# First attention scores two heads at a time on the two halves of TensorE's rows, with the steps of the attention loop in another order

## The chip, the core and the metric

The kernel runs on one core of a Trainium2 chip. The metric is the device time of one execution in microseconds (us). TensorE multiplies matrices and writes PSUM, VectorE (DVE) and ScalarE (ACT) read PSUM and work on rows, GpSimd (POOL) does small vector work, SyncE (SP) issues most DMA transfers. Each engine takes its instructions in program order and waits on semaphores.

## The reference

The block is an adaptive layer norm around an attention layer with an MLP, and then one around a mixture of experts. Cut to what matters here (B = 8 sequences of S = 512 tokens, D = 128, H = 16 heads of 8 elements):

```python
h = _layernorm(x) * (1 + ca) + sa                     # ca, sa, ... from silu(c) @ wmod
x = x + ga * attn_layer(h)                            # ga, gb: clipped gates
h = _layernorm(x) * (1 + cb) + sb
x = x + gb * ffn(h)                                   # shared expert + top 2 of 8 experts

# attn_layer
x = _layernorm(hidden_states, ln1_g, ln1_b)
Q = einsum('bsd,dhr,hre->bhse', x, q_U, q_V) + q_b    # K, V alike
scores = einsum('bhse,bhte->bhst', Q, K) * scale
scores = where(causal, scores, -1e9)
attn = softmax(scores, axis=-1)
ctx = einsum('bhst,bhtd->bhsd', attn, V)
h = hidden_states + ctx @ out_U @ out_V + out_b
return h + gelu(_layernorm(h) @ fc1_U @ fc1_V + fc1_b) @ fc2_U @ fc2_V + fc2_b
```

## The kernel before

**The whole program.** A setup (about the first 42 us of the span) loads and multiplies out the weights and normalises the first three sequences. The attention follows, up to about 381 us. Then come the MLP, the router and the scatter of tokens to expert slots, up to about 538 us, and at last the experts. The diff touches the setup and the attention.

**The attention loop.** A group is 4 of the 16 heads of one sequence, and there are 32 groups (`NG`). Step n works on three groups at once: `s1(n + 3, ...)` makes the first scores of group n+3, `s2(n, ...)` makes the second, transposed scores of group n, and `context(n - 1, ...)` multiplies the probabilities of group n-1 with V. Steps -3, -2 and -1 hold first scores alone, and steps 29 and up hold none. The loops run over `n` in `range(FIRST_STEP, MERGE)` on every engine.

**First scores.** Q and K are each split into bf16 parts, six products are stacked, so that one score is a contraction over 48 rows (`SROWS`). The stacks of Q (`q_st`) and of K (`k_st`) lie on partitions 0 to 47 for one head and 64 to 111 for another. A unit of `S1_UNITS` is one PSUM bank of queries i (128 of them) by all keys up to i: two heads each in units 0 to 3 (128 or 256 keys), one head in units 4 to 11 (384 or 512 keys). For each unit TensorE first writes the causal mask (`ident_b` times `later_q`, L1245) and then adds the scores (L1248), both over all 128 rows: the other head's rows of `q_st` are zero. VectorE takes the row maximum of the bank (`take_max`, L1669). GpSimd splits the negated maxima into three bf16 rows (`split_max`, L831 to L839), TensorE transposes them (`transpose_max`, L1254), ScalarE copies them out (`empty_max`, L1020), and SP stores them to `max_d` (L597) and loads them into three more rows of `q_st` (L607), a step and more ahead of their use.

**Second scores.** `s2(n, u)` has six units, each two PSUM banks of `ps_s2`, and its matmuls stand on 64 rows each: one head on the lower half, one on the upper half, with their own bank (mask L1272, scores L1276). The added rows subtract the maximum. ScalarE takes the exponential of both banks (`exp_unit`, L989). `context` (L1293) uses 32 columns of the array for each of four heads.

**The ring.** The first scores share three PSUM banks (`ps_r`, a ring) with the transposed maxima ("M"), the transposed input ("T"), the projections ("Q", "K", "V"), the output projection ("O") and the transposed rows after attention ("U"). `ring_order` writes the order by hand; entry k lies in bank k modulo 3, and `bank` makes TensorE wait until the entry three places earlier has been read, by VectorE (`max_taken`), or by ScalarE (`act_emptied`). So a bank that ScalarE is late with holds up first scores.

**The other work of a step** goes by n modulo 4, one sequence in four steps: TensorE does O and K in one step, V in the next, U in the next, T and Q in the last. VectorE does one or two parts of the layer norms in each step (`layer_norm`, after units 3 and 7), and adds O after unit 3. `gates` (L1563 and on) works out the gates ga and gb on VectorE after step -3. SP's queue holds, in each step, in this order: the loads of stacks for a coming sequence, `load_ctx`, `store_max`, the stores of stacks, `store_ctx`, `load_max`, `move_rec`. In step 27 (`EARLY_STEP`) SP issues the loads that the MLP and the experts need (L671 to L679).

## Time and profile before

| | us |
|---|---|
| median of three runs | 706.72 |
| lowest and highest of the three | 703.84, 706.77 |
| the profiled execution, its own time | 706.39 |
| its span, first to last instruction | 704.6 |

The granted clock of TensorE was 0.98 over the span. The profile lists for each engine the time in which it was busy. The rows of a timeline are instructions in order of time; consecutive ones of a kind are merged (x4), and the bracket tells how long the engine was idle before and what ended it. A matmul's duration has a fixed part in it, so what one costs in a sequence is read from the distance between the starts. Of the idle reasons, "issue" is time in which the engine waited for nothing that the profile shows.

### The profile page before, as it was taken

The numbers are of one execution on the slowest core, as the hardware profiler recorded it, in microseconds if no ns is written. First come the engines' busy times: TensorE is split into PE (matmuls) and PEld (weight loads), VectorE is DVE, ScalarE is ACT, GpSimd is POOL, SyncE is SP. The second block draws the span as 40 slices with busy tenths as digits, with TensorE's granted clock in tenths as the row PEclk, the third lists the DMA queues.
The fourth block names the chain that finished last, engine by engine and source line by source line (L and its number), as shares of the span: only waits on it lengthen the run. The fifth ranks groups of instructions, "written<-read, shape, count | busy, mean of one in ns | idle before, by whom it ended". The sixth has DMA issues, their size and how long they took to land.

```text
span 704.6 us, 15442 instructions
## 1 busy us (share of the span) xinstructions
PE 633.6 (90%) x5389; PEld 416.6 (59%) x5389; DVE 447.6 (64%) x1346; ACT 409.1 (58%) x720; POOL 301.7 (43%) x480
## 2 busy tenths in 40 slices
PE   4977899999999999999978886999998999999997
PEld 3543444444444544444434575766766999999993
DVE  5749887878788776767742878777673222222227
ACT  4432667676676767666666565676434555555550
POOL 4232424243442524232313438766771545455452
PEclk9999999999999999999999998999899999999999
DMA  9552332443343344332463511211236777777769
GB/s 212 189 177 74 118 102 87 144 138 113 109 153 102 126 140 136 131 106 72 132 189 108 143 36 50 81 51 50 70 96 197 205 239 222 221 224 225 234 209 322
DMA packets 86125, 100.97 MB, mean 143 GB/s; under 512 B 13008, under 2 KB 68216, under 8 KB 85952
## 3 DMA queue, kind: packets, MB, share of 16 engines
q1 hardware_dynamic: 76896, 87.19, 40.3%
q0 software_dynamic: 4544, 9.45, 3.7%
q10 hardware_dynamic: 4608, 3.35, 1.8%
q8 instruction: 43, 0.70, 0.4%
q14 instruction: 34, 0.28, 0.1%
HBM read 60.28 MB, written 37.57 MB: 139 GB/s over the span
## 4 chain that ended last, share of the span: by engine, by line
PE 53%; DVE 14%; DMA 9%; ACT 8%; SPq 6%; issue 5%; POOL 4%; POOLq 0%; ACTq 0%; DVEq 0%
PE ps_pv L1293 9%; PE ps_r L1478 7%; PE ps_s L1468 6%; DVE row_max L1669 6%; PE ps_r L1248 5%; PE ps_r L1245 4%; DMA arena<-slots_d 4%; PE ps_pv L1364 4%; PE ps_s L1276 3%; POOL slots_d L910 3%; PE ps_r L1223 2%; PE ps_s L1272 2%; PE ps_s L1372 2%; ACT arena L1081 2%; DMA arena<-in_w_mod 1%
## 5 line engine op out<-in xcount | busy, mean ns | idle before, releaser
L1669 DVE TENSOR_REDUCE row_max<-ps_r 128x1 f32<-128x384 f32 (+3 forms) x384 | 206.9, 595 | 63.1 <-PE ps_r L1248 61.8
L989 ACT ACTIVATE arena<-ps_s 128x1024 f32<-128x1024 f32 (+1 forms) x192 | 159.3, 881 | 70.8 <-PE ps_s L1276 69.8
L1248 PE MATMUL ps_r<-arena 128*128 128x384 bf16 (+3 forms) x512 | 118.7, 303 | 0.0
L956 POOL DMA_INDIRECT y_d<-arena,target x78 | 74.9, 960 | 87.7 <-DVE arena L1878 75.5
L1245 PE MATMUL ps_r<-later_q,ident_b 128*128 128x128 bf16 (+1 forms) x384 | 91.4, 244 | 22.0 <-DVE row_max L1669 15.8
L1245 PEld LDWEIGHTS ps_r<-later_q,ident_b 128*128 128x128 bf16 x384 | 35.9, 97 | 84.1 <-DVE row_max L1669 42.4
L1874 DVE TENSOR_TENSOR arena<-ps_r,arena_early 128x256 f32<-128x256 f32 x39 | 16.6, 425 | 108.2 <-PE ps_r L1478 108.2
L1293 PE MATMUL ps_pv<-arena 128*32 128x512 f32 (+3 forms) x1024 | 83.3, 443 | 0.1
L910 POOL DMA_INDIRECT slots_d<-arena,slots x64 | 65.5, 1023 | 18.2 <-issue 18.2
L1276 PE MATMUL ps_s<-arena 51*128 51x256 bf16 (+3 forms) x512 | 59.9, 298 | 0.0
L1478 PEld LDWEIGHTS ps_r<-arena 128*128 128x128 f32 x480 | 58.2, 192 | 1.5
L1144 ACT ACTIVATE arena<-ps_s,arena 128x256 f32<-128x256 f32 x120 | 50.4, 471 | 13.9 <-PE ps_s L1468 13.2
L1478 PE MATMUL ps_r<-arena 128*128 128x128 f32 x480 | 58.3, 275 | 0.0
L1248 PEld LDWEIGHTS ps_r<-arena 128*128 128x128 bf16 x512 | 50.6, 99 | 12.8 <-issue 2.4
L1468 PE MATMUL ps_s<-arena 128*128 128x256 f32 x240 | 56.8, 379 | 0.0
L831 POOL TENSOR_SCALAR neg_part<-row_max 128x16 bf16<-128x16 f32 x32 | 8.3, 260 | 89.0 <-DVE row_max L1669 89.0
L1293 PEld LDWEIGHTS ps_pv<-arena 128*32 128x32 f32 x1024 | 27.0, 110 | 32.2 <-issue 25.8
L1468 PEld LDWEIGHTS ps_s<-arena 128*128 128x128 f32 x240 | 43.3, 190 | 4.6
L1272 PE MATMUL ps_s<-ident_h,lower_k 64*128 64x64 bf16 (+1 forms) x384 | 39.9, 204 | 5.2 <-ACT arena L989 4.7
L1102 ACT ACTIVATE arena<-ps_s,cols 128x512 f32<-128x512 f32 x32 | 21.6, 686 | 31.6 <-PE ps_s L1372 30.9
L770 POOL TENSOR_TENSOR var_eps<-moments,ln_eps 128x4 f32<-128x4 f32 x24 | 4.9, 203 | 79.9 <-DVE moments L1494 79.9
L1272 PE MATMUL ps_s<-ident_h,upper_k 64*128 64x64 bf16 (+1 forms) x384 | 38.7, 198 | 0.0
(236 smaller groups left out, 1129.1 us busy)
## 6 DMA issues: line engine op xcount, KB each, us to landing
arena<-in_ew SPq DMA_DIRECT2D x30, 514.0 KB
ctx_d<-ctx_raw SPq DMA_DIRECT2D x32, 256.0 KB, 3.1
arena<-q_d SPq DMA_DIRECT2D x64, 102.0 KB
arena<-k_d SPq DMA_DIRECT2D x64, 96.0 KB
arena<-slots_d SPq DMA_DIRECT2D x39, 132.0 KB, 3.1
arena_early<-in_ew SPq DMA_DIRECT2D x9, 514.0 KB
arena<-y_d SPq DMA_DIRECT2D x8, 512.0 KB, 6.0
q_d<-arena_early SPq DMA_DIRECT2D x8, 384.0 KB, 2.9
```

What stands on the lines that cost most here:

```text
L910: pool.indirect_dma_start(slots_d[:], bass.IndirectOffsetOnAxis(ap=slots[:, c, i:i + 1], axis=0), n3x[:, c, i, :], None).then_inc(scattere ...
L956: pool.indirect_dma_start(y_d[:], bass.IndirectOffsetOnAxis(ap=target[:, k, c:c + 1], axis=0), res[:, k, c, :], None).then_inc(put[k], 16)
L989: act.activation(dst, src, ACT.Exp, scale=SCALE).then_inc(exp_done, 1)
L1144: act.activation(x_hidden[:, k, f], ps_s2[:, 2 * (k % 2) + f // 2, (f % 2) * SLOTS:(f % 2 + 1) * SLOTS], ACT.Relu, bias=x_w[k][:, FF + NF ...
L1245: pe.matmul(diag, ident_b[:], later_q[:].unsqueeze(1).to_broadcast([P, len(js), P]), start=True, stop=False, skip_group_check=True)
L1248: mm = pe.matmul(bnk[:, k * keys:(k + 1) * keys], q_st[b % 2][:, g, j, i * P:(i + 1) * P], k_st[b % 2][:, g, j // 2, 0:keys], start=False, ...
L1272: pe.matmul(banks[half][:, :, at:at + HALF], stationary[whole], near, start=(at == 0), stop=False, skip_group_check=True)
L1276: mm = pe.matmul(banks[j % 2][:, k // 2, :], k_st[b % 2][rows, g, j // 2, kt * P:(kt + 1) * P], q_st[b % 2][rows, g, j, kt * P:S], start=F ...
L1293: mm = pe.matmul(ps_pv[32 * j:32 * j + 32, kt * P:S], v_sb[b % 2][:, kt, GROUPS * j + g, :], probs[:, p % 2, at:at + length], start=(kt == ...
L1468: mm = pe.matmul(ps_s2[:, 2 * (k % 2) + f // 2, (f % 2) * SLOTS:(f % 2 + 1) * SLOTS], x_w[k][:, f * P:(f + 1) * P], tok_t[:, k], start=Tru ...
L1478: mm = pe.matmul(ps_s1[:, k % 2, c * P:(c + 1) * P], x_hidden[:, k, f, c * P:(c + 1) * P], x_w[k][:, FF + f * D:FF + (f + 1) * D], start=( ...
L1669: dve.reduce_max(row_max[:, m % 2, js[0] % 2, j:j + len(js), i], src, AXIS.X).then_inc(max_taken, 1)
```

## The change

**First scores in pairs.** `s1` now makes two units at once, one on the rows 0 to 63 and one on the rows 64 to 127 of the array, each into its own bank of the ring. The mask is made of four products on 64 rows (`ident_h` with the two parts of a wider `later_q`), the scores follow by turns of the two halves. `q_st` holds no zero rows any longer (`JH` becomes 2), so that their clearing on ScalarE, on SP's queue (two DMAs of `zeros`) and the wait for both fall away.

**Ring and places.** "M" leaves the ring for a corner of `ps_s2` (bank 3), and so do V, Q and K of all sequences but the first, and U of the first six (`beside`, the right half of the banks 2 and 3). Products beside the ring wait in `place_of` for what lay there, and the unit 1 of the second scores waits until ScalarE has emptied them. T stands after the units 4 and 5, O after 6 and 7.

**Order of a step.** Each pair of first scores is followed by one unit of the second scores and a part of the context. ScalarE's, VectorE's (layer norm after units 1, 3, 7 and 9, O after 7) and GpSimd's orders follow, the roots (`x_rstd_of`, `h_rstd_of`) now ahead of K's remainder. `gates` moves into VectorE's setup.

**Unread products.** `fill_in` issues two products of 512 bf16 columns ahead of each pair in the steps -3 to -1; nobody reads them.

```diff
+def beside(name, b):
+    return b is not None and (name == "V" or name in "QK" and b > 0 or name == "U" and GROUPS * b + AFTER_T_AT < NG)
...
-        units(m, 0, 1)
-        one(n, "O")
-        units(m, 2, 3)
-        if 0 <= m - 1 < NG:
-            order.append(("M", m - 1))
-        units(m, 4, 5)
-        one(n, "T", "K", "V")
-        units(m, 6, 7)
-        one(n, "Q")
-        units(m, 8, 9, 10, 11)
-        if batch_at(n, AFTER_T_AT) is not None:
-            order.append(("U", batch_at(n, AFTER_T_AT)))
+        units(m, 0, 1, 2, 3, 4, 5)
+        one(n, "T")
+        units(m, 6, 7)
+        one(n, "O")
+        units(m, 8, 9)
+        one(n, *(name for name in "QKU" if not beside(name, batch_at(n, AT[name]))))
+        units(m, 10, 11)
...
-        q_st = [first.take(GROUPS, JH, S, dt=BF16) for k in range(2)]
+        q_st = [first.take(GROUPS, 2, S, dt=BF16) for k in range(2)]
...
+            def home(name, b):
+                if beside(name, b):
+                    return ps_s2[:, 2:4, S // 2:S]
+                return ring(name, b).rearrange("p (c s) -> p c s", c=2)
...
-                    for k in range(2):
-                        sp.dma_start(q_d[k, len(PRODUCTS)].rearrange("p (c s) -> p c s", c=2),
-                                     zeros[:].bitcast(BF16).unsqueeze(1).to_broadcast([P, 2, S // 2])).then_inc(zero_rows, 16)
...
-                    for stack in q_st:
-                        act.activation(stack[:].rearrange("p g j s -> p (g j s)").bitcast(F32), zeros[:, 0:1].to_broadcast([P, GROUPS * JH * S // 2]), ACT.Copy)\
...
+                    def place_of(name, b):
+                        if not beside(name, b):
+                            bank(name, b)
+                            return home(name, b)
+                        n = GROUPS * b + AT[name]
+                        pe.wait_ge(small_copied, 4)
+                        wait(pe, act_emptied, beside_until(n))
+                        wait(pe, max_copied, min(n + LAG, NG))
+                        wait(pe, exp_done, NS2 * n + 4)
+                        return home(name, b)
...
+                    def fill_in(n):
+                        if -LAG <= n < 0:
+                            for k in range(2):
+                                pe.matmul(ps_pv[:].rearrange("p (c s) -> p c s", c=NT), ident_b[:],
+                                          lower_q.unsqueeze(1).to_broadcast([P, NT, P]), start=True, stop=True)
...
-                            bnk = bank("S", n)
-                            keys = P * (i + 1)
-                            diag = bnk[:, 0:len(js) * keys].rearrange("p (j s) -> p j s", j=len(js))[:, :, keys - P:keys]
-                            pe.matmul(diag, ident_b[:], later_q[:].unsqueeze(1).to_broadcast([P, len(js), P]), start=True, stop=False,
-                                      skip_group_check=True)
+                            banks = [bank("S", NS1 * m + u + half)[:, 0:len(js) * keys].rearrange("p (j s) -> p j s", s=keys) for half in range(2)]
+                            for stationary, at in ((lower_q, keys - P), (upper_q, keys - HALF)):
+                                for half in range(2):
+                                    whole = slice(HALF * half, HALF * half + HALF)
+                                    near = ident_h[whole].unsqueeze(1).to_broadcast([HALF, len(js), HALF])
+                                    pe.matmul(banks[half][:, :, at:at + HALF], stationary[whole], near, start=(at == keys - P), stop=False,
+                                              skip_group_check=True)
                             for k, j in enumerate(js):
-                                mm = pe.matmul(bnk[:, k * keys:(k + 1) * keys], q_st[b % 2][:, g, j, i * P:(i + 1) * P],
-                                               k_st[b % 2][:, g, j // 2, 0:keys], start=False, stop=True, skip_group_check=True)
-                            mm.then_inc(s1_done, 1)
+                                for half in range(2):
+                                    rows = slice(HALF * half, HALF * half + SROWS)
+                                    mm = pe.matmul(banks[half][:, k, :], q_st[b % 2][rows, g, j // 2, i * P:(i + 1) * P],
+                                                   k_st[b % 2][rows, g, j // 2, 0:keys], start=False, stop=True, skip_group_check=True)
+                                    if k == len(js) - 1:
+                                        mm.then_inc(s1_done, 1)
...
+                        if u == 1:
+                            wait(pe, max_copied, min(n + LAG - 1, NG))
+                            wait(pe, act_emptied, beside_until(n))
...
-                        s2(n, 0)
-                        s2(n, 1)
-                        context(n - 1, 0)
-                        s1(m, 0, 1)
+                        fill_in(n)
+                        s1(m, 0, 1)
+                        s2(n, 0)
+                        context(n - 1, 0)
+                        fill_in(n)
+                        s1(m, 2, 3)
+                        s2(n, 1)
+                        context(n - 1, 1)
...
                     normalise_all(2)
+                    gates()
...
-                            if u in (3, 7):
+                            if u in (1, 3, 7, 9):
                                 layer_norm(n, u)
...
-                        if n == MOD_STEP - 1:
-                            gates()
```

**TensorE at the head of a step, before.** `ps_s` is `ps_s2`, `arena` the stacks or probabilities; `128x64` is the output tile, and the bracket holds what the instruction waits for. The rows are a step's first two units of the second scores, the first part of the context and the first unit of first scores.

```order
L1272 MATMUL ps_s<-ident_h,lower_k 128x64 [waits exp_done,max_loaded1]
...
L1276 MATMUL ps_s<-arena 128x512 x2
L1272 MATMUL ps_s<-ident_h,lower_k 128x64 [waits exp_done]
...
L1276 MATMUL ps_s<-arena 128x512 x2
L1293 MATMUL ps_pv<-arena 32x512 [waits act_emptied,ctx_out,exp_done]
...
L1245 MATMUL ps_r<-later_q,ident_b 128x256 [waits max_taken,st_loaded0]
L1248 MATMUL ps_r<-arena 128x128 x2
```

The same place now, the second step of a sequence:

```order
L1289 MATMUL ps_r<-ident_h,later_q 128x2x64 [waits max_taken,st_loaded1]
...
L1294 MATMUL ps_r<-arena 128x128 x4
L1330 MATMUL ps_s<-ident_h,later_k 128x64 [waits exp_done,max_loaded0]
...
L1334 MATMUL ps_s<-arena 128x512 x2
L1351 MATMUL ps_pv<-arena 32x512 [waits ctx_out,exp_done]
...
L1289 MATMUL ps_r<-ident_h,later_q 128x2x64 [waits max_taken]
...
L1294 MATMUL ps_r<-arena 128x256 x4
L1330 MATMUL ps_s<-ident_h,later_k 128x64 [waits act_emptied,max_copied,exp_done]
```

A pair of first scores now stands ahead of each single unit of the second scores, and the second of these waits for ScalarE's emptying too.

**TensorE around the transposed maxima and K's or V's projection, before.** L1254 transposes the maxima, L1229 is V's projection.

```order
L1254 MATMUL ps_r<-ident_b,neg_part 48x128 [waits max_taken,max_split]
L1245 MATMUL ps_r<-later_q,ident_b 128x128 [waits max_taken]
L1248 MATMUL ps_r<-arena 128x384
...
L1229 MATMUL ps_r<-w_qkv,arena_early 128x128 [waits act_emptied]
...
L1276 MATMUL ps_s<-arena 128x256 x4
...
L1276 MATMUL ps_s<-arena 128x128 x4
L1245 MATMUL ps_r<-later_q,ident_b 128x128 [waits act_emptied]
L1248 MATMUL ps_r<-arena 128x512
```

Now (L1308 transposes the maxima, L1264 is V's projection):

```order
L1308 MATMUL ps_s<-ident_b,neg_part 48x128 [waits exp_done,act_emptied,max_copied,max_split]
...
L1334 MATMUL ps_s<-arena 128x384 x2
...
L1294 MATMUL ps_r<-arena 128x512 x2
...
L1334 MATMUL ps_s<-arena 128x256 x4
L1264 MATMUL ps_s<-w_qkv,arena_early 128x128 [waits exp_done,max_copied,act_emptied,small_copied]
...
L1289 MATMUL ps_r<-ident_h,later_q 128x64 [waits max_taken]
...
L1294 MATMUL ps_r<-arena 128x512 x2
...
L1334 MATMUL ps_s<-arena 128x128 x4
```

The maxima and the projection write `ps_s` in place of `ps_r`; the first scores behind the projection no longer wait for ScalarE.

**TensorE ahead of the first of all first scores, before** (L1223 is Q's or K's projection of the second sequence, L1203 the bias of the output):

```order
L1223 MATMUL ps_r<-arena_early,w_qkv 128x512 [waits act_emptied]
L1203 MATMUL ps_r<-w_out,arena 128x128 [waits act_emptied,small_copied]
L1245 MATMUL ps_r<-later_q,ident_b 128x256 [waits st_loaded0,v_ones,act_emptied,mod_copied,small_copied]
L1248 MATMUL ps_r<-arena 128x128 x2
L1245 MATMUL ps_r<-later_q,ident_b 128x256 [waits dve_emptied]
```

Now:

```order
L1257 MATMUL ps_s<-arena_early,w_qkv 128x256 [waits small_copied,act_emptied]
...
L1223 MATMUL ps_r<-w_out,arena 128x128 [waits act_emptied,small_copied]
L1257 MATMUL ps_s<-arena_early,w_qkv 128x256 [waits act_emptied,small_copied]
...
L1271 MATMUL ps_pv<-later_q,ident_b 128x512 [waits v_ones,mod_copied,small_copied]
...
L1289 MATMUL ps_r<-ident_h,later_q 128x2x64 [waits act_emptied,st_loaded0]
...
L1294 MATMUL ps_r<-arena 128x128 x4
```

K's projection now waits for ScalarE to empty Q's, since both lie in the same place, and two unread products stand ahead of the pair.

## Rows read from the trace of the kernel before

**Rows 1.** The page, first part, and busy time by stretch (two of attention, its end):

```profile
PE 633.6 (90%) x5389; PEld 416.6 (59%) x5389; DVE 447.6 (64%) x1346; ACT 409.1 (58%) x720; POOL 301.7 (43%) x480
...
180.00:200.00 20.00, 19.06 (x207) 9.20 (x206) 15.89 (x39) 14.83 (x24) 10.09 (x16) 1.00 0.41 137
200.00:220.00 20.00, 18.06 (x218) 9.39 (x214) 17.22 (x49) 11.97 (x18) 6.25 (x17) 1.00 0.37 124
...
360.00:380.00 20.00, 15.57 (x207) 6.99 (x199) 1.67 (x5) 14.52 (x21) 3.54 (x4) 0.91 0.40 131
```

**Rows 2.** The chain that ended last: the context's later parts in steps 1, 8, 18, 27:

```profile
81.30 1.43 PE ps_pv L1293 x24
...
150.78 1.43 PE ps_pv L1293 x24
...
253.26 1.43 PE ps_pv L1293 x24
...
342.17 1.43 PE ps_pv L1293 x24
```

**Rows 3.** Waits between 80 and 270 us: engine line, waited for, us, times, longest:

```profile
DVE row_max L1669 <- PE ps_r L1248: 34.8, 55, 1.8
...
PEld ps_r L1245 <- DVE row_max L1669: 21.8, 46, 1.1
```

**Rows 4.** Timeline of TensorE, first scores: two units of 256, two of 512 keys:

```profile
190.86 0.27 PE L1245 MATMUL ps_r<-later_q,ident_b 128*128 128x256 bf16 x1
...
191.19 0.27 PE L1245 MATMUL ps_r<-later_q,ident_b 128*128 128x256 bf16 x1
...
196.74 0.23 PE L1245 MATMUL ps_r<-later_q,ident_b 128*128 128x128 bf16 x1 [0.26 <-ACT arena_early L1005]
...
197.02 0.22 PE L1245 MATMUL ps_r<-later_q,ident_b 128*128 128x128 bf16 x1
```

**Rows 5.** Timeline of TensorE, second scores: starts of units in the same steps:

```profile
195.75 0.23 PE L1272 MATMUL ps_s<-ident_h,lower_k 64*128 64x128 bf16 x2
...
196.09 0.22 PE L1272 MATMUL ps_s<-ident_h,lower_k 64*128 64x128 bf16 x2
...
198.35 0.20 PE L1272 MATMUL ps_s<-ident_h,lower_k 64*128 64x64 bf16 x2
...
198.64 0.19 PE L1272 MATMUL ps_s<-ident_h,lower_k 64*128 64x64 bf16 x2
```

**Rows 6.** Timeline of TensorE, from second scores to the context:

```profile
198.70 0.38 PE L1276 MATMUL ps_s<-arena 51*128 51x512 bf16 x2
...
199.01 1.06 PE L1293 MATMUL ps_pv<-arena 128*32 128x512 f32 x8
```

**Rows 7.** Timeline of VectorE, the twelve maxima of one step:

```profile
349.43 0.76 DVE L1669 TENSOR_REDUCE row_max<-ps_r 128x2 f32<-128x256 f32 x2 [0.73 <-PE ps_r L1248]
350.93 1.29 DVE L1669 TENSOR_REDUCE row_max<-ps_r 128x2 f32<-128x512 f32 x2 [0.74 <-PE ps_r L1248]
...
353.73 4.57 DVE L1669 TENSOR_REDUCE row_max<-ps_r 128x1 f32<-128x384 f32 x8 [0.92 <-PE ps_r L1248]
```

**Rows 8.** Timeline of GpSimd in steps 23 and 24:

```profile
310.11 1.28 POOL L857 TENSOR_TENSOR ctx_n<-ctx_t,rec_rows 128x512 f32<-128x512 f32 x1 [6.89 <-DMA rec_rows<-rec_d]
...
315.08 0.25 POOL L839 TENSOR_SCALAR neg_part<-neg_left 128x16 bf16<-128x16 f32 x1
```

**Rows 9.** Timeline of SP's queue from step 27 on:

```profile
344.10 0.32 SPq L597 DMA_DIRECT2D max_d<-max_rows  x1
...
347.12 6.69 SPq L673 DMA_DIRECT2D arena_early<-mod_d  x3
353.85 1.65 SPq L675 DMA_DIRECT2D arena_early<-in_router_t  x1
...
357.51 0.83 SPq L597 DMA_DIRECT2D max_d<-max_rows  x1
...
362.61 0.58 SPq L607 DMA_DIRECT2D arena<-max_d  x2
```

**Rows 10.** Waits between 340 and 384 us:

```profile
PEld ps_s L1272 <- DMA arena<-max_d: 3.0, 1, 3.0
```

**Rows 11.** Timeline around VectorE's gates, in the steps of first scores alone:

```profile
53.80 0.52 DVE L1574 SCALAR_TENSOR_TENSOR arena<-arena 8x128 f32<-8x128 f32 x2
...
54.72 0.28 PE L1245 MATMUL ps_r<-later_q,ident_b 128*128 128x256 bf16 x1 [1.57 <-DVE row_max L1669]
```

## What is expected of the change

> **What bounds the kernel now.** I read four views in this order.
>
> First the page and the busy time by stretch: in the attention TensorE is busy for 19.06 and 18.06 of 20 us, VectorE for 15.89 and 17.22, ScalarE for less, and the clock is granted in full (1.00) [rows 1]. So TensorE is nearly full and VectorE is close behind: (15.89 + 17.22) / 40 = 0.83 of the time.
>
> Second the chain, which gives the length of a step: the context's later parts start at 81.30 us in step 1, 150.78 in step 8, 253.26 in step 18 and 342.17 in step 27 [rows 2]. That is 69.5 / 7 = 9.93 us a step, then 102.5 / 10 = 10.25, then 88.9 / 9 = 9.88. VectorE's work is thus 0.83 x 10.25 = 8.5 us in the middle steps. In the last ones, which have no input norms, it is at least its twelve maxima, 0.76 + 1.29 + 4.57 = 6.6 us [rows 7]. That the steps hardly became shorter when the input norms ended shows that TensorE sets their length.
>
> Third the waits: between 80 and 270 us VectorE waits for first scores for 34.8 us, and TensorE's first scores for VectorE for 21.8 us [rows 3]. Both happen, since the work comes in lumps: neither engine is saturated all the time.
>
> Fourth SP's queue. In step 27 it issues loads for the later phases from 347.12 us on (6.69 and 1.65 us for two of them). The store of maxima behind them goes out at 357.51 and their load at 362.61 [rows 9], and TensorE waits 3.0 us for it [rows 10]. From there on the queue sets the pace.
>
> Everything behind the attention (some 325 us) is untouched, and starts when the attention ends.
>
> **The change part by part.** The sum is made against the profiled execution's own time, 706.39 us (span 704.6); that is 0.33 us under the median of the three runs, so the same sum holds for both.
>
> *First scores in pairs.* A unit of 256 keys takes 191.19 - 190.86 = 0.33 us for 768 columns, one of 512 keys 0.28 us for 640 [rows 4], so 0.43 ns a column. A step's twelve units have 7168 columns: 3.1 us. A pair now has just the shape of a unit of the second scores, and those run two heads side by side already: 0.34 us with 256 keys (two matmuls on each half and the masks), 0.29 us with 512 [rows 5]. The 384 key pairs by the same rate take 0.23, the 128 key pair 0.25. Six pairs: 0.25 + 0.34 + 2 x 0.23 + 2 x 0.29 = 1.6 us. TensorE is relieved of 1.5 us a step.
>
> *More changes of shape.* The array goes between 128 rows, 64 rows and 32 columns. The second 512-column pair starts at 198.70, streams for 0.21, and the context starts at 199.01 [rows 6]: a gap of 0.10 us. Before, a step has 8 such changes; now the second scores follow the first without one, but the context is cut into three, and the maxima, O and the projections stand alone: some 10.7. That costs 0.27 us a step. The Trainium skill, page "TensorEngine Tiling (Array Packing)", section "Key Properties", says that changing the tiling mode drains TensorE. By that rule, the trace agrees, with 0.10 us. It speaks against this part of the change.
>
> Net relief on TensorE: 1.2 us a step. The steps 0 to 26 can pass it on (27 steps, 32 us at most); from 27 on the queue decides.
>
> *What is late next.* In the middle steps (8 to 17) TensorE needs 10.25 - 1.2 = 9.05, VectorE 8.5. They meet at short distance now: a pair takes two of three banks, so TensorE can start the next pair when VectorE has read the first bank of the last one, and no sooner. Behind the first pair stand one unit (0.29), the context's longest part (1.06, [rows 6]), two changes (0.2) and the next pair (0.34), 1.9 us, while VectorE has 0.76 of maxima and some 0.6 of norm: it idles for about 0.5. T or O in the ring costs about as much again in every second step. 8.5 + 0.5 + 0.3 = 9.3. Taken: 9.3, a gain of 0.95 in 10 steps. Bounds: 8.5 (VectorE full) and 10.25 (nothing).
>
> *Sum over the steps.* Steps 0 to 7: 8 x 1.2 = 9.6. Steps 8 to 17: 10 x 0.95 = 9.5. Steps 18 to 26, VectorE relieved of the input norms: 9 x 1.2 = 10.8. Together 29.9 us.
>
> *GpSimd's chain.* In steps 23 and 24 GpSimd waits for the reciprocals' rows until 310.11, does three operations of 1.3 us, and has the maxima split at 315.08 + 0.25 [rows 8]. This hangs on SP's queue, not on TensorE. With shorter steps the transposition comes first and waits: -2.5 us. Elsewhere the same chain ends some 3 us sooner and is covered.
>
> *The steps of first scores alone.* These three run at VectorE's pace. The gates leave it there, ending at 53.80 + 0.52, for which TensorE had waited 1.57 us [rows 11]; they now fall into the setup, where VectorE waited for TensorE anyway. The unread products (2 x 512 columns, 0.43 us a pair at the rate above, 0.86 at half clock) run while VectorE reads two banks (0.76 to 1.3 us): nothing, or 0.2 a pair if the clock is low. Against it K's projection now waits for Q's emptying, and the first pair starts about 1 us later. Together +0.5, between -3 and +3.
>
> *Edits at nothing.* The two clearings of `q_st` on ScalarE and the two DMAs of zeros lie beside weight loads that come sooner in the queue. The emptying of Q, K, V and U (up to 1.4 us) comes after the last exponential, and the second unit that waits for it stands some 2 us into the next step: hidden. If it is not, it costs what is over in each step. M out of the ring frees first scores from ScalarE. The roots ahead of K's remainder: 1.2 us on GpSimd, which is idle more than half the time.
>
> *From step 27 on.* Maxima of the last groups, SP's loads, store, load: 344.10 to 364 us stays as it is, and a faster loop only reaches it sooner. No gain and no loss.
>
> 29.9 - 2.5 + 0.5 = 27.9. 706.4 - 27.9 = 678.5; taken 679.
>
> **The rivals.**
>
> *The exchange of banks takes most of it.* If each of the six pairs, not only the first, lets VectorE idle for 0.25 us, a middle step takes 8.5 + 1.5 = 10.0, and the others gain 0.3: 27 x 0.28 = 7.5, so 699. For it: the 34.8 us of VectorE's waits now, with up to three banks of lead [rows 3]. Against it: TensorE has 1.2 us less to do, and the norms are spread over four places. The Trainium skill, the same page, section "PSUM Bottleneck", says that after a speedup of TensorE the reading of PSUM may become the bottleneck; by that rule, the trace agrees with 0.83 for VectorE.
>
> *Chains through SP and GpSimd take a part.* The 2.5 us come in each sequence, or the emptying of Q and K holds the second unit: -10 in all, 689.
>
> *The waits vanish as well.* Order and work are spread evenly, VectorE is full in the middle (8.6), and the late steps fall to 8.0: 8 x 1.9 + 10 x 1.65 + 9 x 1.9 = 49 at the utmost; 45 less gives 661.
>
> *Slower: the clock falls.* TensorE has less to do in a step, and the clock is granted at half (1.2 GHz) after it has waited: the stretch with the 3.0 us wait shows 0.91, and the attention, whose waits end at 1.8 us, shows 1.00 [rows 1, 3, 10]. A step's 8.4 us of TensorE would take 16.8 at half clock, 7.5 more than 9.3. Four of 27 steps at half clock eat the gain; that is the point from which it decides. Seven of them: 679 + 52 = 731. Against it: what is left idle comes in pieces of under 1 us.
>
> *Pairs do not overlap.* Then first scores stay at 3.1 or more and the changes of shape and the 24 mask products add 0.4 us a step: 706.4 + 11 = 717. The second scores speak against it [rows 5].
>
> **How the numbers follow.** Forecast (672 to 686) 0.50; exchange of banks (690 to 703) 0.17; chains (686 to 696) 0.10; waits vanish (656 to 670) 0.12; clock 0.08; no overlap 0.03. The range reaches from 662, in the middle of the fourth, to 700, over the second: about 0.8. A measurement of this kernel can tell about 0.5% (3.5 us) from no change. Faster by more: 0.50 + 0.15 + 0.10 + 0.12 = 0.87; within: 0.04; slower: 0.09.
>
> **What would show it.** In the profile after: starts of 512 key pairs 0.29 us apart from what follows, halves at the same time; six context starts a step with 0.1 us gaps; steps of 8.7, 9.3 and 8.7 us; VectorE busy over 0.9 in the middle steps; a granted clock of 1.00 from 65 us on; one wait of 2 to 3 us of the transposed maxima for GpSimd about step 24; the wait for the loaded maxima in step 30 as before or longer. Wrong would be: VectorE's waits for first scores over 1.5 us a step (the exchange of banks), second scores waiting for ScalarE's emptying, or a clock under 1.00 in the loop.

## The result

Twenty executions of the changed kernel took 705.01 us in the median (693.1 to 712.0), twenty of the kernel before on the same chip 706.78 (703.8 to 713.2). The changed kernel's executions spread more widely, and the comparison leaves out those more than 1.5% above the fastest of a kernel, eleven of the changed kernel's twenty and none of the other's: by it the changed kernel takes 0.9877 of the time before, interval 0.985 to 0.990, some 9 us less. A later comparison on another chip gave 0.9874 (0.984 to 0.991), with medians of all its executions of 700.6 and 708.9 us, so the gain does not hang on which executions are counted. The forecast was 679 us, 28 us less, with 662 to 700 as the range: the direction was right, the size was three times too large.

The profiled execution took 706.2 us and lies above its own median. A second one, of the later comparison, has a span of 697.8 us. What is read below stands in both, unless it says otherwise. Line numbers of the changed kernel: first scores L1289 (masks) and L1294, second scores L1330 and L1334, context L1351, transposed maxima L1308, maxima on VectorE L1735, reciprocals L1758.

The page of the changed kernel (busy time; the clock in 40 slices), and busy time by stretch, whose last columns are granted clock, DMA share and GB/s; they answer to [rows 1]:

```profile
PE 607.5 (86%) x5841; PEld 401.2 (57%) x5841; DVE 450.2 (64%) x1346; ACT 408.1 (58%) x718; POOL 301.2 (43%) x478
...
PEclk9999799999999989998989988999899999999999
...
180.00:200.00 20.00, 18.23 (x252) 9.12 (x246) 16.56 (x41) 15.62 (x23) 10.54 (x17) 0.95 0.43 140
200.00:220.00 20.00, 17.20 (x267) 8.64 (x265) 18.73 (x52) 14.44 (x21) 6.41 (x17) 1.00 0.38 124
360.00:380.00 20.00, 13.16 (x164) 4.92 (x168) 1.28 (x4) 14.13 (x20) 1.08 (x1) 0.83 0.36 124
```

TensorE is busy for 26 us less, and in an undisturbed stretch (200 to 220 us) VectorE is busy for 18.73 of 20 us. But the clock is under 1.00 in stretches of the loop, which it was not before.

TensorE's timeline in step 13, two pairs and the context behind the first (answers to [rows 4 to 6]):

```profile
196.40 0.29 PE L1289 MATMUL ps_r<-ident_h,later_q 64*128 64x128 bf16 x4 [0.65 <-DVE row_max L1735]
...
196.62 0.24 PE L1330 MATMUL ps_s<-ident_h,later_k 64*128 64x64 bf16 x4
196.68 0.40 PE L1334 MATMUL ps_s<-arena 51*128 51x512 bf16 x2
197.01 1.06 PE L1351 MATMUL ps_pv<-arena 128*32 128x512 f32 x8
...
204.29 0.23 PE L1289 MATMUL ps_r<-ident_h,later_q 64*128 64x64 bf16 x4
...
204.58 0.28 PE L1330 MATMUL ps_s<-ident_h,later_k 64*128 64x128 bf16 x4
```

A pair of 128 keys takes 196.62 - 196.40 = 0.22 us until the second scores behind it start, a pair of 512 keys 204.58 - 204.29 = 0.29. The prediction had 0.25 and 0.29. The gap at the change of shape ahead of the context is again 0.1 us.

The waits between 80 and 270 us (answers to [rows 3]):

```profile
PEld ps_r L1289 <- DVE row_max L1735: 48.6, 72, 4.3
...
DVE row_max L1735 <- PE ps_r L1294: 20.9, 36, 2.1
...
DVE recs L1758 <- DMA sums<-ctx_d: 7.4, 3, 3.7
```

TensorE, by the rows of its weight loads (`PEld`), now waits for VectorE for 48.6 us instead of 21.8, once for 4.3. VectorE waits less for TensorE, 20.9 instead of 34.8. The third row is new in size: the reciprocals' wait for the context's sums was 2.4 us between 80 and 330 us before, at most 0.9 at once. (In the second execution it is 3.9 between 80 and 270 us, at most 2.0.)

The steps tell the rest. By the starts of the context (L1351, 128x512), 18 of the steps 1 to 27 of the profiled execution take 8.4 to 9.7 us; but step 1 takes 10.1, step 11 13.7, step 19 15.7, step 24 12.3. In the second execution other steps are long: step 7 13.2, step 12 12.4, step 24 12.3. Here is step 19, SP's queue, then VectorE, then TensorE, in the first execution:

```profile
247.68 0.54 SPq L609 DMA_DIRECT2D arena<-q_d  x1
...
253.18 0.60 SPq L612 DMA_DIRECT2D arena<-k_d  x1
253.88 0.57 SPq L646 DMA_DIRECT2D sums<-ctx_d  x1
...
251.98 0.69 DVE L1735 TENSOR_REDUCE row_max<-ps_r 128x1 f32<-128x512 f32 x1 [0.32 <-PE ps_r L1294]
256.38 0.55 DVE L1758 RECIPROCAL recs<-sums 128x64 f32<-128x64 f32 x1 [3.71 <-DMA sums<-ctx_d]
...
257.95 0.39 PE L1289 MATMUL ps_r<-ident_h,later_q 64*128 64x128 bf16 x4 [3.46 <-DVE row_max L1735]
259.24 1.50 PE L1351 MATMUL ps_pv<-arena 128*32 128x384 f32 x8
```

SP issues eight loads of the stacks, from 247.68 on, before it issues the load of the sums at 253.88. VectorE meets the reciprocals early, since steps are shorter, and stands for 3.71 us with a maximum behind it. TensorE's pair waits for that maximum for 3.46 us. Then the context's second part takes 1.50 us instead of 0.85: the clock is at half (1.2 GHz). So a load on SP's queue, which the prediction had read from step 27 on alone, costs a step some 6.5 us.

### The profile page after: what moved, and what is told of

It is laid out like the page before. It is cut to its first block, busy times and chain, and to the rows that moved or that the text cites. A ratio compares the mean times of both kernels' runs of the same rounds, so it can differ in the third digit from the quotient of the medians.

```text
span 704.5 us, 16609 instructions
## 1 busy us (share of the span) xinstructions
PE 607.5 (86%) x5841; PEld 401.2 (57%) x5841; DVE 450.2 (64%) x1346; ACT 408.1 (58%) x718; POOL 301.2 (43%) x478
## 4 chain that ended last, share of the span: by engine, by line
PE 46%; DMA 13%; DVE 12%; SPq 9%; issue 9%; ACT 6%; POOL 5%; POOLq 0%; ACTq 0%; DVEq 0%
PE ps_r L1543 7%; PE ps_s L1533 7%; PE ps_pv L1351 6%; DVE row_max L1735 6%; PE ps_pv L1429 4%; DMA arena<-slots_d 3%; PE ps_r L1289 3%; POOL slots_d L931 3%; PE ps_r L1294 3%; DMA k_d<-arena_early 2%; DMA arena<-y_d 2%; PE ps_s L1334 2%; SPq L612 2%; PE ps_s L1437 2%; SPq L609 2%
## 5 line engine op out<-in xcount | busy, mean ns | idle before, releaser
L1735 DVE TENSOR_REDUCE row_max<-ps_r 128x1 f32<-128x384 f32 (+3 forms) x384 | 211.4, 594 | 45.8 <-PE ps_r L1294 43.1
L1007 ACT ACTIVATE arena<-ps_s 128x1024 f32<-128x1024 f32 (+1 forms) x192 | 168.6, 882 | 86.8 <-PE ps_s L1334 85.1
L1351 PE MATMUL ps_pv<-arena 128*32 128x512 f32 (+3 forms) x1024 | 95.4, 471 | 0.0
L1289 PEld LDWEIGHTS ps_r<-ident_h,later_q 64*128 64x128 bf16 x768 | 24.7, 94 | 121.3 <-DVE row_max L1735 78.9
L1289 PE MATMUL ps_r<-ident_h,later_q 64*128 64x64 bf16 (+1 forms) x768 | 49.5, 206 | 42.7 <-DVE row_max L1735 42.3
L1938 DVE TENSOR_TENSOR arena<-ps_r,arena_early 128x256 f32<-128x256 f32 x39 | 16.6, 425 | 108.2 <-PE ps_r L1543 108.2
L1294 PE MATMUL ps_r<-arena 48*128 48x384 bf16 (+3 forms) x512 | 70.8, 310 | 0.0
L1334 PE MATMUL ps_s<-arena 51*128 51x256 bf16 (+3 forms) x512 | 70.6, 310 | 0.0
L1164 ACT ACTIVATE arena<-ps_s,arena 128x256 f32<-128x256 f32 x120 | 50.4, 471 | 13.8 <-PE ps_s L1533 13.2
L1330 PE MATMUL ps_s<-ident_h,later_k 64*128 64x64 bf16 (+1 forms) x768 | 49.2, 204 | 6.0 <-ACT max_rows L1038 4.9
L1330 PEld LDWEIGHTS ps_s<-ident_h,later_k 64*128 64x128 bf16 x768 | 35.9, 98 | 25.1 <-ACT arena L1007 10.2
L1351 PEld LDWEIGHTS ps_pv<-arena 128*32 128x32 f32 x1024 | 24.3, 111 | 29.9 <-issue 16.5
L878 POOL TENSOR_TENSOR ctx_n<-ctx_t,rec_rows 128x512 f32<-128x512 f32 x8 | 10.2, 1275 | 61.7 <-DMA rec_rows<-rec_d 61.7
```

What stands on the lines that cost most here:

```text
L1007: act.activation(dst, src, ACT.Exp, scale=SCALE).then_inc(exp_done, 1)
L1164: act.activation(x_hidden[:, k, f], ps_s2[:, 2 * (k % 2) + f // 2, (f % 2) * SLOTS:(f % 2 + 1) * SLOTS], ACT.Relu, bias=x_w[k][:, FF + NF ...
L1289: pe.matmul(banks[half][:, :, at:at + HALF], stationary[whole], near, start=(at == keys - P), stop=False, skip_group_check=True)
L1294: mm = pe.matmul(banks[half][:, k, :], q_st[b % 2][rows, g, j // 2, i * P:(i + 1) * P], k_st[b % 2][rows, g, j // 2, 0:keys], start=False, ...
L1330: pe.matmul(banks[half][:, :, at:at + HALF], stationary[whole], near, start=(at == 0), stop=False, skip_group_check=True)
L1334: mm = pe.matmul(banks[j % 2][:, k // 2, :], k_st[b % 2][rows, g, j // 2, kt * P:(kt + 1) * P], q_st[b % 2][rows, g, j // 2, kt * P:S], st ...
```

## The experiments

The theory after these rows: every undisturbed step gains about what was forecast. The gain is given back at waits behind orders written for longer steps (SP's queue, GpSimd's), and each wait is made dearer by a clock that falls behind it. The main rival: the clock falls because pairs leave TensorE less busy, whatever waits.

**Loads in another order.** The load of the sums moves ahead of the stack loads in SP's step, in the changed kernel and in the kernel before:

```
+                        if batch_at(n, CTX_AT) is not None:
+                            load_ctx(batch_at(n, CTX_AT))
                         for g, later in ((0, 0), (1, 0), (2, 1), (3, 2)):
...
-                        if batch_at(n, CTX_AT) is not None:
-                            load_ctx(batch_at(n, CTX_AT))
```

> The changed kernel with one edit: SP's queue issues the context's loads (load_ctx) ahead of the eight loads of stacks in the same step. Theory Q (the queue): in the changed kernel VectorE waits at its reciprocal for the sums (2.8, 3.7 and 2.4 us in steps 10, 18 and 22), the last two maxima of the step stand behind it, TensorE waits for those, and the granted clock falls after it. By Q these three waits and the falls behind them go: the contexts' starts in steps 11/12 and 19/20 lie under 10 us apart, not 13.7 and 15.7, and the ratio to the kernel before falls from 0.988 to 0.970 to 0.978. Rival C (the clock falls by itself, from TensorE's smaller load): the waits go, but the steps still hold stretches at half clock, and the ratio stays at 0.983 or above.

> The kernel before with the same edit of SP's queue. Theory Q: there the sums came in time (waits of 0.3 us), so the edit changes nothing: ratio 0.997 to 1.003. Rival (the queue's order was a cost in both kernels): ratio under 0.995.

Measured: 0.9851 (0.980 to 0.990) for the changed kernel, 1.0037 (1.001 to 1.007) for the one before. Step 19 falls to 10.4 us and the reciprocals wait no more. But step 15 now takes 14.5, the clock is at half for as long as before (41 us between 60 and 380 us), and the ratio is the one that the rival had named (0.983 or above). The kernel before became slightly slower with the edit. In the changed kernel with that order, ScalarE and TensorE:

```profile
220.77 0.60 ACT L1043 ACTIVATE ctx_raw<-ps_pv 128x512 f32<-128x512 f32 x1 [3.26 <-DMA ctx_d<-ctx_raw]
...
222.09 0.29 PE L1289 MATMUL ps_r<-ident_h,later_q 64*128 64x64 bf16 x4 [3.23 <-ACT arena_early L1014]
```

The store of the context now stands at the end of the longer row of transfers; ScalarE's copy waits for it, the emptying of T behind the copy, and TensorE behind that. So the queue's order as a whole has to be tested.

**SP's order mended.** The store of the context goes ahead of the loads too:

```
                         if batch_at(n, CTX_AT) is not None:
                             load_ctx(batch_at(n, CTX_AT))
+                        if 0 <= n - 2 < NG:
+                            store_ctx(n - 2)
                         for g, later in ((0, 0), (1, 0), (2, 1), (3, 2)):
```

> The changed kernel, in which SyncE issues in each step first the load of the context's row sums, then the store of the context of two steps before, and only then the stack loads, the maxima's store and load. Theory (each undisturbed step is won, and the gain is lost again to waits behind an in-order queue, each of about 3 us, that drag the granted clock down after them): with the loads first gone, the stall moved from step 19 (15.7 us) to step 15 (14.5 us), because the context's store then stood behind a longer row of transfers; with the store ahead too, both should be gone: no step but 12, 24 and those from 29 on over 11 us, TensorE's longest wait on VectorE and on ScalarE's x_t copy under 1.5 us each between 90 and 300 us, half clock in the loop 25 to 35 us instead of 40.8, ratio to the kernel before 0.975 to 0.985. Rival (the clock falls because pairs leave TensorE less busy, whatever waits): half clock stays at 35 us or more, ratio 0.985 to 0.990, as with the loads first alone (0.9851).

Measured: 0.9763 (0.971 to 0.982), 690.6 us. Both stalls are gone: steps 1 to 27 take 8.2 to 11.5 us, and TensorE's longest wait for VectorE between 80 and 330 us is 1.6, where it was 3.5. By the records of the granted clock, the attention loop runs 20 us at half instead of 41. TensorE's work is the same, so the falls that went stood behind the waits. The rival is not refuted: the clock still falls for 6.8 us in step 0 and for 3.4 us at 133 us, where no wait is long.

**GpSimd's order.** The addition of the output bias moves a step earlier: `batch_at(n, 3)` becomes `batch_at(n, 2)`.

> The changed kernel, with GpSimd's addition of the output bias (line 900) in the step before, instead of the step whose GpSimd work also holds the normalised context and the addition of fc2's bias, and whose splitting of the maxima it delays. Theory: the transposition of the negated maxima no longer waits 2.6 us in step 24 but under 1, step 24 takes 9 to 10.5 us instead of 12.4 and the half clock behind it (6.8 us from 313 us on) goes; step 19 stays at about 15.7 us; ratio 0.981 to 0.986, 1 to 4 us less than the changed kernel. Rival (the bias addition is not what delays the split, the load of the reciprocals is): step 24 over 11.5 us, ratio 0.986 to 0.989.

Measured: 0.9824 (0.978 to 0.987), which overlaps the interval of the changed kernel without the move. Step 24 takes 10.4 us instead of 12.3, though step 23 took 12.7, behind a wait of 3.0 us for the sums, and step 19, which was expected to stay long, took 9.9. What the move takes away is seen in step 12 of the changed kernel's second execution, GpSimd, then TensorE:

```profile
184.62 1.28 POOL L878 TENSOR_TENSOR ctx_n<-ctx_t,rec_rows 128x512 f32<-128x512 f32 x1 [7.78 <-DMA rec_rows<-rec_d]
185.86 1.27 POOL L893 TENSOR_TENSOR h_sb<-h_sb,fc_bias 128x512 f32<-128x512 f32 x1
187.10 1.27 POOL L900 TENSOR_TENSOR h_sb<-h_sb,out_bias 128x512 f32<-128x512 f32 x1
...
189.61 0.25 POOL L860 TENSOR_SCALAR neg_part<-neg_left 128x16 bf16<-128x16 f32 x1
...
189.92 0.24 PE L1308 MATMUL ps_s<-ident_b,neg_part 128*48 128x128 bf16 x1 [1.34 <-POOL neg_part L860]
```

This is the chain of [rows 8], and in the changed kernel it reaches TensorE in step 12 as well, where before it was covered.

**All moves, in both kernels, and a third.** To both moves comes `EARLY_STEP = NG - 6` (SP's loads for the later layers in step 26).

> The changed kernel with three moves: SyncE's order of the run before this one, GpSimd's addition of the output bias one step earlier, and SyncE's loads for the later layers in step 26 instead of 27. Theory: the three causes of lost gain are gone together; no step from 1 to 26 over 11 us, 27 steps in 250 to 256 us (before 271, changed kernel 266), half clock inside the loop under 20 us, and the tail from step 27 on 2 to 5 us shorter; ratio to the kernel before 0.955 to 0.970. Rival (the clock falls by lighter load): half clock in the loop stays above 35 us, ratio 0.975 to 0.985. Rival 2 (SyncE's queue is full in the tail wherever the loads stand): the tail's long steps only move, ratio 0.970 to 0.978.

> The kernel before with the same three moves. Theory (the queue order costs only since the steps have become shorter): steps 1 to 26 as before, since its waits there were hidden behind TensorE; ratio 0.990 to 1.003, the part below 1 from the earlier loads in the tail and the transposition that waited for GpSimd in step 24. Rival (the moves are good by themselves, whatever the pairs do): ratio 0.975 to 0.985, so that the gap between the two kernels stays at 1.2% under the same moves.

Measured: 0.9731 (0.969 to 0.978) and 1.0069 (1.005 to 1.009). The third move was a miss: step 28, which stands behind its loads, took 15.0 us in the changed kernel and 16.6 in the kernel before. (Step 20 of the changed kernel took 14.6, behind GpSimd's chain, whose rows came 10.1 us late; that step lies six steps ahead of the moved loads.) SP's queue in the changed kernel with the three moves:

```profile
333.67 6.73 SPq L696 DMA_DIRECT2D arena_early<-mod_d  x3
...
350.24 0.57 SPq L630 DMA_DIRECT2D arena<-max_d  x2
```

The maxima that now stand behind the loads are needed sooner. Without the third move, and with it one step later instead:

> The changed kernel with the two moves that each gained alone: SyncE issues the load of the context's sums and the store of the context ahead of the stack loads (0.9763 alone), and GpSimd adds the output bias one step earlier (0.9824 alone); the loads for the later layers stay in step 27. Theory: what SyncE's order left, the transposition that waits for GpSimd in steps 12 and 24 (10.7 and 11.2 us), goes to 9 to 10 us; no step from 1 to 27 over 11 us; ratio to the kernel before 0.965 to 0.975, 1 to 6 us under SyncE's order alone, and below the three moves together (0.9731), whose loads in step 26 made steps of 14.6 and 15.0 us. Rival (the two moves take away the same time): ratio 0.974 to 0.980.

> The kernel before with SyncE's and GpSimd's moves alone, without the earlier loads that made one step of 16.6 us in the kernel before with all three. Theory (the moves pay only where steps are shorter): ratio 0.994 to 1.004, so that the paired scores under the same moves are worth 2.0 to 3.0% instead of 1.2%. Rival (the moves are good in themselves): ratio 0.980 to 0.990.

> The kernel with the two moves, and SyncE's loads for the later layers in step 28 instead of 27. Theory (the row of loads takes 6 to 7 us of SyncE's queue wherever it stands, and the maxima's transfers behind it hold up the steps from 29 on): the long step moves by one and keeps its 11 to 15 us, or moves behind the last load of maxima, where nothing waits for it; the time is within 3 us of the two moves alone, on either side. Rival (the loads cost only where maxima still have to be moved): 3 to 6 us less than with the two moves.

The changed kernel with the two moves takes 0.9737 (0.970 to 0.977), 689.8 us; the kernel before with the same two 1.0012 (0.998 to 1.005). So the two moves are worth 1.4% in the changed kernel and nothing in the one before: what they take away was hidden there. So the third move changed nothing in the changed kernel's time (0.9731 against 0.9737): it moved the long step. With the late loads in step 28 the ratio is 0.978 (0.975 to 0.981), and step 30 takes 12.9 us instead of 8.0: the queue's load of the maxima is late one step further on.

**The clock at the start.** In step 0 of the changed kernel TensorE waits 0.3 to 1.3 us ahead of each pair, and the clock falls:

```profile
60.00:80.00 20.00, 15.44 (x158) 7.90 (x158) 17.69 (x43) 8.68 (x14) 6.01 (x14) 0.82 0.25 79
...
73.08 0.29 PE L1289 MATMUL ps_r<-ident_h,later_q 64*128 64x64 bf16 x4 [1.26 <-DVE row_max L1735]
...
75.72 2.05 PE L1257 MATMUL ps_s<-arena_early,w_qkv 128*128 128x256 f32 x4
```

Three runs with fewer or more unread products. The first is the changed kernel without them; the second the changed kernel with one more ahead of each pair in all steps from 0 on, into the pair's first bank; the third has the two products in step 0 too, on top of the two moves:

```
 # first                       # third
-if -LAG <= n < 0:            -if -LAG <= n < 0:
+if False:                    +if -LAG <= n <= 0:
 # second, in s1
+near_bank = bank("S", NS1 * m + u)
+if m >= LAG:
+    pe.matmul(near_bank.rearrange("p (c s) -> p c s", c=NT), ident_b[:],
+              lower_q.unsqueeze(1).to_broadcast([P, NT, P]), start=True, stop=True)
```

> The changed kernel without the unread products of the three steps of first scores alone (36 pairs' products of 512 columns fewer). If they hold the clock there, as the granted 1.00 from 40 to 60 us suggests, it falls to half for 3 to 10 us between 44 and 68 us, at a price of 1 to 4 us (ratio 0.990 to 0.994). Rival: VectorE sets the pace there, and the ratio stays within 0.986 to 0.990.

> The changed kernel with one more unread product: from step 0 on, ahead of each pair of first scores, once the first of its two banks is free and before the wait for the second, 128 x 512 bf16 columns into that first bank (0.21 us at full clock, 6 a step). Rival C: TensorE's light load lets the clock fall; with the unread products the stretches at half clock in the loop (some 41 us between 60 and 380 us) become fewer than half, and the ratio falls from 0.988 to 0.975 to 0.983. Theory Q: the clock falls behind a wait of 3 us, which one product cannot bridge; the stretches stay, and the products cost what does not fit into waits: ratio 0.988 to 1.000.

> The kernel with the two moves, and the two unread products ahead of each pair in step 0 too, as in the three steps of first scores alone. It computes nothing more. Theory: in step 0 TensorE has gaps of 0.3 to 1.3 us ahead of its pairs and the clock is at half from about 70 to 80 us; with the products the clock stays at 1.00 there, the first context starts at 76 to 79 us instead of 80.4, and the kernel takes 1 to 4 us less than without them (ratio 0.962 to 0.972). Rival (the products take time on the path, as they did in every step of the loop): the first context starts at 80.5 us or later and the ratio is that of the two moves or 0.003 more.

Measured: 0.9942 (0.991 to 0.997) without any, where the clock is 0.50 from 40 to 80 us and the first context starts at 83.5 us instead of 80.4. One product ahead of each pair in the loop: 1.0109 (1.007 to 1.015). It does keep the clock (1.00 between 80 and 330 us), which the theory had not expected, and no wait of TensorE there is over 1.2 us. But steps take 9.2 to 11.6 us: from a product's start to that of its pair it is 0.33 us (204.92 to 205.25 in this run), on the path even where TensorE would not have waited. Whether the clock stayed because TensorE has more to do or because longer steps leave the queues time, this run does not separate. In step 0 alone: 0.965 (0.961 to 0.969), 683.1 us, the best of all. The stretch of step 0 in its second run:

```profile
60.00:80.00 20.00, 17.35 (x188) 7.80 (x190) 18.44 (x45) 10.14 (x15) 6.75 (x15) 1.00 0.27 84
...
75.24 1.10 PE L1257 MATMUL ps_s<-arena_early,w_qkv 128*128 128x256 f32 x4
```

Is that gain separate from the moves?

> The changed kernel with the two unread products ahead of each pair in step 0 too, and no other move. The products in step 0 took 6 us off the kernel with the two moves. Theory (two separate losses: half clock that starts in step 0, and waits behind SyncE's and GpSimd's orders): here too step 0 keeps its full clock and the first context starts about 1 us earlier, but steps 11, 19 and 24 keep their stalls of 12 to 15 us; ratio to the kernel before 0.979 to 0.985, 3 to 6 us under the changed kernel. Rival 1 (the stalls are chance meetings that depend on when step 0 ends, and the shift by 1 us alone removes them): ratio under 0.975. Rival 2 (the gain of the products only comes where the queues are free): ratio 0.985 to 0.990.

> The changed kernel with the two moves and the products in step 0, once more with more rounds, beside the kernel with the products alone. Ratio to the kernel before 0.962 to 0.970, no step but 28 over 10 us, no half clock between 60 and 330 us. Rival (part of the first result was chance, since the half clock comes at other places in other executions): 0.970 to 0.976.

> The changed kernel with SyncE's order and the two unread products in step 0, GpSimd's bias where it was. Theory (GpSimd's move gained 1.2% alone, but 0.3% on top of SyncE's, and it let a 128x512 operation of GpSimd fall on VectorE's norm in one step): 0.966 to 0.972, within 3 us of the kernel with all of them (0.965 and 0.968). Rival (the bias holds up the transposition in steps 12 and 24 as soon as steps are short): 0.973 to 0.978.

Measured: the products in step 0 alone 0.9889 (0.985 to 0.993), no better than the changed kernel; with the two moves again 0.968 (0.964 to 0.972), 683.9 us; with SP's move alone 0.9701 (0.966 to 0.974). The products alone were expected to gain (0.979 to 0.985), so it fits the second rival: what is saved in step 0 shows only where the queues are mended. A time of its own for GpSimd's move is not shown: step 24 takes 9.5 to 9.7 us with it and 11.2 without, but the intervals overlap.

**The price of a late maximum.** Five more maxima of one bank (3.05 us) in steps 6, 11, 16 and 21, into unread columns, in the kernel with the two moves and in the one with the products too:

```
+                        if u == 10 and m - LAG in (6, 11, 16, 21):
+                            for k in range(5):
+                                dve.reduce_max(idle_max[:, m - LAG - 2 + k:m - LAG - 1 + k], src, AXIS.X)
```

> The kernel with the two moves, and in steps 6, 11, 16 and 21 five more maxima of the same 128x512 bank by VectorE into unread columns, ahead of the eleventh maximum (row_max of 0.6 us each, so that TensorE's next pair waits some 3 us longer); it measures what one late maximum of VectorE costs. Theory (a stall drags the clock down behind it): each of the four makes its step 4.5 to 8 us longer, 3 us of waiting and 1.5 to 5 us of half clock after it, 13.7 to 15.7 us a step as in the changed kernel's steps 11 and 19; 18 to 30 us in all over the two moves alone. Rival 1 (the clock has nothing to do with the waits): 3 us each, 10 to 13 us in all, with no half clock behind them. Rival 2 (later steps catch up): under 8 us in all.

> The kernel of the run before with the five more maxima in steps 6, 11, 16 and 21, as in the earlier run with such maxima; there each cost 3.5 us beside a kernel that had half clock in its loop anyway. Here the clock is full until 330 us without them. Theory: a late maximum of 3 us costs its 3 us and the half clock behind it (3.4 to 6.8 us at half, worth 1 to 2 us), 4 to 5 us each, 16 to 20 us in all. Rival 1 (the clock at half costs nothing beyond the wait): 11 to 13 us. Rival 2 (the fall of the clock needs the earlier one in step 0): full clock until 330 us, and 11 to 13 us.

Measured: 0.9927 against 0.9737, and 0.9915 against 0.968. By the medians that is 13.8 / 4 = 3.5 us for one, and 18.3 / 4 = 4.6 where the clock had been full. The first lies nearest to its rival of 3 us, the second in the theory's range. By the ratios it is 3.4 and 4.2, each uncertain by almost 1 us. The starts of the contexts settle it: in the second kernel a step with the late maximum and the step behind it take 4.7, 4.5, 4.5 and 4.9 us more than the same two steps without; in the first it is 3.4, 1.0, 5.5 and 5.8, little where the clock fell at that place in any case (133 and 184 us). VectorE and TensorE in step 6 of the second:

```profile
131.39 3.05 DVE L1738 TENSOR_REDUCE idle_max<-ps_r 128x1 f32<-128x512 f32 x5
...
135.19 0.40 PE L1290 MATMUL ps_r<-ident_h,later_q 64*128 64x128 bf16 x4 [3.63 <-DVE row_max L1739]
136.26 1.93 PE L1352 MATMUL ps_pv<-arena 128*32 128x512 f32 x8
139.34 0.85 PE L1352 MATMUL ps_pv<-arena 128*32 128x384 f32 x8
```

After a wait of 3.63 us the context's first part takes 1.93 us instead of 1.06, the next is back at full clock. Busy time between 80 and 330 us, without and with the late maxima:

```profile
80.00:330.00 250.00, 218.05 (x3288) 108.44 (x3283) 217.94 (x523) 191.15 (x269) 98.07 (x208) 0.99 0.40 128
...
80.00:330.00 250.00, 209.19 (x3058) 102.97 (x3054) 215.69 (x518) 178.91 (x251) 93.97 (x196) 0.96 0.37 119
```

By the records of the granted clock behind these means, 3.4 and 20.5 us are at half, 17 us more. The Trainium skill, page "TensorE: Matmul & The Clock Gate", section "HAM oscillation — how this bites in real kernels", says that work in bursts with waits between them starts each burst at half clock, and counts half of that time as lost. By that, 8.5 us; the trace agrees roughly, with 18.3 - 4 x 3.05 = 6.1.

**The changed kernel itself, again.**

> The changed kernel itself, once more, for a second profiled execution of it and its time beside the kernel that follows. Its twenty executions so far lay between 693 and 712 us. Theory (its stalls come from the orders of the queues): the waits of VectorE's reciprocals for the context's sums are there again, 5 to 10 us in the loop, with steps 11, 19 or 24 over 12 us, in this execution as in the first; ratio to the kernel before 0.985 to 0.992. Rival (the stalls of the first profile were an accident of that execution): no step over 11.5 us and a time near 693 us.

Measured: 0.9874 (0.984 to 0.991), median 700.6 us. The stalls are there (the GpSimd rows above are of this execution), at other steps; step 19, long in the first, takes 10.4. So they are no accident of the first profile, but which step meets which queue differs from one execution to the next; that would explain why its times spread.

## Why the forecast was wrong

Point by point, by the steps of the prediction.

*First scores in pairs, changes of shape.* Right for the pairs and the gap that the rows of step 13 show.

*The length of an undisturbed step.* Right in the middle, too hopeful at both ends. The context's starts in steps 1, 8, 18 and 27, first of the changed kernel's second execution, then of the kernel with two moves and products in step 0:

```profile
79.97 1.06 PE L1351 MATMUL ps_pv<-arena 128*32 128x512 f32 x8
...
147.13 1.06 PE L1351 MATMUL ps_pv<-arena 128*32 128x512 f32 x8
...
245.15 1.07 PE L1351 MATMUL ps_pv<-arena 128*32 128x512 f32 x8
...
333.13 1.07 PE L1351 MATMUL ps_pv<-arena 128*32 128x512 f32 x8
```

```profile
79.31 1.06 PE L1351 MATMUL ps_pv<-arena 128*32 128x512 f32 x8
...
142.55 1.06 PE L1351 MATMUL ps_pv<-arena 128*32 128x512 f32 x8
...
235.58 1.07 PE L1351 MATMUL ps_pv<-arena 128*32 128x512 f32 x8
...
315.92 1.07 PE L1351 MATMUL ps_pv<-arena 128*32 128x512 f32 x8
```

The second gives 63.24 / 7 = 9.03 us a step, 93.03 / 10 = 9.30 and 80.34 / 9 = 8.93. The forecast was 8.7, 9.3 and 8.7. In the middle it is met, and by its own terms:

```profile
142.55:235.58 93.03, 82.03 (x1216) 41.83 (x1214) 85.24 (x226) 72.82 (x104) 43.29 (x85) 1.00 0.43 141
```

VectorE, the third number of busy time, works 8.5 us a step there and is idle for 0.8, as the prediction had it (8.5 + 0.5 + 0.3). At the ends TensorE did not pass on its whole relief of 1.2 us: by the same starts the kernel before takes 9.81, 10.33 and 9.88, so the gains are 0.8, 1.0 and 0.95 where 1.2, 0.95 and 1.2 were forecast, some 4 us too much over these 26 steps. There TensorE is busy for 0.86 and 0.87 of the time and VectorE for 0.90 and 0.83: neither is full, and the waits for each other, which the prediction counted in the middle alone, remain. The changed kernel as it was gives 9.59, 9.80 and 9.78 in its second execution. From step 1 to 27 the kernel before takes 260.9 us, the changed one 253.2 (257.5 in its first execution), the mended one 236.6: of the 24.3 us that are there to be had, 7.7 arrived (3.4 in the first).

*SP's queue in the loop.* The step of the prediction that failed. It read this queue from step 27 on alone; for the loop its sum had no term for it, only a rival, "Chains through SP and GpSimd take a part", with 10 us and a chance of 0.10. The two moves gave back 0.9874 - 0.9737 = 1.4%, 9.7 us: the rival's size, but in part by luck, since it had named the rows of GpSimd's chain and the emptying of Q and K, and most of it came from the loads of the sums and the store of the context, which SP's order alone mended (0.9763). The row that would have told was the reciprocals' wait for the sums: in four waits 2.4 us, up to 0.9, in the kernel before. A wait that short means that the load lands just in time; every shorter step makes it longer.

*GpSimd's chain.* Too small, for the same reason. The prediction gave it 2.5 us in step 24, where TensorE waited 2.3 us in both executions, and said that elsewhere it "ends some 3 us sooner and is covered". But the cover shrinks with every shorter step between the batch's loads and this chain. In the second execution the chain reached TensorE in step 12 (1.3 us) and step 20 (1.1 us) too.

*The clock.* The prediction set half clock apart, as a case in which whole steps run at half, with a chance of 0.08. It came in short stretches instead, 41 us of the attention loop in one execution and 34 in the other, by the records of the granted clock, where the kernel before had 3. Of these, 24 and 17 us stand at a wait of TensorE of 1.34 to 4.91 us. That was not a rule: a wait of 2.2 us at 299 us of the first execution brought no fall. The other 17 us in each have no wait over 1.26 us ahead: they lie in step 0, near 133 us and near 343 us, and the one at 134 us of the first execution follows waits of 0.24, 0.52 and 0.65 us. So "Against it: what is left idle comes in pieces of under 1 us" was true of undisturbed steps and no protection there, and for this part the rival of the lighter load stands. What sets the fall near 133 us stays open. It is no accident of one execution: of the twelve profiled ones of the changed kernel with any order of the queues, and with or without the products in step 0, eight have a fall between 131 and 135 us, and three others one at 97 or 98.

A reading was wrong too. The prediction took the 1.8 us of [rows 3] for waits that leave the clock at 1.00, but that row is VectorE's; TensorE's own longest was 1.1. And in the kernel before, right behind TensorE's wait of 1.57 us [rows 11], the clock was already at half for 3.4 us:

```profile
55.00:60.00 5.00, 4.54 (x23) 1.92 (x20) 4.85 (x9) 0.27 (x1) 0.00 (x0) 0.66 0.40 118
```

*The steps of first scores alone.* Forecast +0.5, measured +1.6 and +2.0 us (first context at 80.0 and 80.4 instead of 78.3). The clearest part is step 0 at half clock; with products there it is +0.3 and +1.0. But the kernel before with other orders of the queues had its first context at 79.3 to 79.9, so a miss of this size is not clear of the spread. The unread products in the three steps before it do what they should: without them all of it is at half clock.

*From step 27 on.* Forecast 0. From step 27 to 32 the kernel before takes 38.7 us, the changed one 41.4 and 40.9. The queue sets the pace, as forecast; SP's queue and the chain of the changed kernel:

```profile
346.62 7.00 SPq L696 DMA_DIRECT2D arena_early<-mod_d  x3
...
362.69 0.57 SPq L630 DMA_DIRECT2D arena<-max_d  x2
...
366.51 1.86 PE ps_pv L1351 x8
```

The load of the maxima goes out at 362.69 (362.61 before, [rows 9]), but TensorE's wait there became longer (4.9 and 4.1 us instead of 2.8), and the clock was at half for 6.8 us around it, instead of 3.4 (the context's first part, 1.86 us in the last row, is 1.06 at full clock).

*The sum.* 28 us forecast. 9 arrived; SP's and GpSimd's orders took 10, half clock from step 0 on 4 to 6 on top of that, by the ratios 0.965 and 0.968. The rest, 3 to 5, is about what the steps at both ends fell short by; the parts of the queues and of the clock are uncertain by 3 to 4 us each. The first two can be mended without touching the paired scores: the kernel with both moves and the products in step 0 takes 683 to 684 us on two chips, where the kernel before takes 708.

## What to carry to other kernels

When a change shortens the loop, list every wait that the other queues of the loop now hide, with its margin, and take the shortening times the number of steps off each: a wait of 0.9 us for a load is the next bottleneck. Mend the order of the queues together with the change: here the change alone paid a third of what was forecast, and the two moves alone paid nothing. Price a stall of a busy TensorE above its length, since the clock may fall with it: here 4.6 us for 3. And do not take short waits alone as proof that the clock stays up.

## What was not expected of the hardware

An operation of VectorE with two inputs in SBUF stood still while GpSimd worked. GpSimd, then VectorE, in the changed kernel with the two moves, where they met in step 11:

```profile
180.39 1.27 POOL L878 TENSOR_TENSOR ctx_n<-ctx_t,rec_rows 128x512 f32<-128x512 f32 x1 [5.00 <-DMA rec_rows<-rec_d]
181.62 1.31 POOL L893 TENSOR_TENSOR h_sb<-h_sb,fc_bias 128x512 f32<-128x512 f32 x1
...
178.67 0.60 DVE L1582 SCALAR_TENSOR_TENSOR h_sb<-arena_early,rstd 128x128 f32<-128x128 f32 x2
...
180.39 2.69 DVE L1582 SCALAR_TENSOR_TENSOR h_sb<-arena_early,rstd 128x128 f32<-128x128 f32 x2
```

The same two operations take 0.60 us at 178.67 and 2.69 at 180.39, as long as GpSimd's two. The maximum behind them came late, TensorE waited 2.66 us, and the clock fell: the step took 11.6 us. The maxima, which read PSUM, were not slowed where GpSimd worked beside them: one of 512 keys took at most 0.69 us with such an operation of GpSimd beside it and without. The Trainium skill, page "SBUF — State Buffer", section "Who interferes with whom", says that such an operation of VectorE and one of GpSimd that reads SBUF exclude each other for a whole instruction; the trace agrees. The two operations of GpSimd that met it here are not the moved one, and such meetings stand elsewhere too: in step 7 of the changed kernel's second execution (two operations of VectorE in 1.62 us at 144.16) and in the kernel before (two in 1.51 us at 74.60). So the meeting is a chance of the timing, and not shown to come from the move.
